# Final scatters of layer 2 moved to the pass boundaries, and the records' chain moved into the layer-0 block

## What is computed

```python
def _L0_gnn_ref(x, edge_index, edge_attr, W1, b1, W2, b2, Ws, bs, Wn, bn):
    h = relu(edge_attr @ W1.T + b1);  w = h @ W2.T + b2
    agg = segment_sum(w * x[src], dst)
    return relu(x @ Ws.T + bs + agg @ Wn.T + bn)

def _L1_gnn_ref(x, edge_index):                 # K = 10
    for _ in range(K):
        out = segment_sum(out[col] * w[:, None], row) * BETA + h * ALPHA
    return out / theta

def _L2_gnn_ref(x, edge_index):                 # K = 16, with self loops
    for _ in range(K):
        h = (1.0 - ALPHA) * segment_sum(norm * h[row], col) + ALPHA * x
    return h

def _L3_gnn_ref(x, edge_index, W1, b1, W2, b2, prelu_a):
    h = prelu(gcn_conv(x, W1, b1));  return prelu(gcn_conv(h, W2, b2))
```

## Time and profile before

| what | us |
|---|---|
| median of three runs | 11760.09 (11758.58 to 11783.25) |
| the profiled execution | 11771.36, span 11769.3 |
| PE busy | 4162.7 (35%) |
| DVE busy | 4557.7 (39%) |
| ACT busy | 3757.8 (32%) |
| POOL busy | 7378.6 (63%) |
| granted TensorE clock, mean | 0.561 |

### The profile page before, as it was taken

One profiled execution on the slowest core, in us unless ns is written; L12 is line 12 of the kernel. 1 busy time (PEld: TensorE's weight loads), 2 busy tenths in 40 slices (PEclk: granted clock), 3 DMA queues, 4 the chain that ended last, 5 costly groups with the idle time before them and its releaser, 6 DMA issues. The chain is left out here.

```text
span 11769.3 us, 85659 instructions
## 1 busy us (share of the span) xinstructions
PE 4162.7 (35%) x18774; PEld 3132.2 (27%) x18774; DVE 4557.7 (39%) x11458; ACT 3757.8 (32%) x11422; POOL 7378.6 (63%) x7464
## 2 busy tenths in 40 slices
PE   6860134333333333310333433333333332213433
PEld 4640033222222222210222222222222221112432
DVE  6970033333333334530344444444444432333334
ACT  6960034322222222363322222232222221143322
POOL 6877742666666666655566666666666666654455
PEclk8765555555555555555555555555555555555555
DMA  6561114333333333331333333333333332222211
GB/s 116 155 124 14 28 39 72 85 87 89 91 89 84 88 87 86 85 87 40 80 90 89 91 89 90 93 96 93 96 94 93 93 93 71 67 57 55 59 34 31
DMA packets 904311, 941.00 MB, mean 80 GB/s; under 512 B 378210, under 2 KB 789500, under 8 KB 903708
## 3 DMA queue, kind: packets, MB, share of 16 engines
q1 hardware_dynamic: 677870, 612.09, 17.8%
q0 software_dynamic: 225792, 323.35, 14.8%
q10 hardware_dynamic: 144, 0.10, 0.0%
HBM read 553.87 MB, written 408.86 MB: 82 GB/s over the span
## 5 line engine op out<-in xcount | busy, mean ns | idle before, releaser
L1655 POOL DMA_INDIRECT l_g<-tab,l x4704 | 4624.9, 983 | 2554.7 <-issue 1367.5
L1855 DVE TENSOR_TENSOR_SCAN l_w<-l_m,l_w,bank 96x512 f32<-96x512 bf16 x1248 | 1590.2, 1274 | 4380.1 <-remote 2758.8
L1692 PE MATMUL bank<-ident,l_w 96*128 96x96 f32 x5096 | 1089.1, 363 | 2419.3 <-DVE l_w L1855 1992.3
L1755 ACT ACTIVATE l_o<-l_o,coef_d 128x96 f32<-128x96 f32 x2940 | 856.7, 363 | 3187.2 <-DVE l_o L1883 1603.1
L1681 PE MATMUL bank<-ident,l_g 128*96 128x128 f32 x5096 | 1257.0, 396 | 1360.9 <-DMA l_g<-tab,l 603.1
L1692 PEld LDWEIGHTS bank<-ident,l_w 96*128 96x128 f32 x5096 | 844.8, 222 | 2714.3 <-DVE l_w L1855 2163.8
L1681 PEld LDWEIGHTS bank<-ident,l_g 128*96 128x96 f32 x5096 | 906.9, 189 | 1740.0 <-DMA l_g<-tab,l 645.1
L1751 ACT ACTIVATE l_o<-bank,coef_s 128x96 f32<-128x96 f32 x1764 | 452.4, 345 | 1838.2 <-remote 1114.1
L275 PE MATMUL bank<-tail_up,v 96*96 96x500 f32 (+1 forms) x298 | 296.3, 1098 | 1168.5 <-issue 944.2
L312 PE MATMUL bank<-ident,tail_up 96*125 96x96 f32 (+1 forms) x596 | 159.3, 422 | 780.6 <-issue 468.6
L1891 DVE TENSOR_TENSOR T<-l_o,XS 128x384 f32<-128x384 f32 x735 | 401.2, 546 | 10.7 <-ACT l_o L1755 10.7
(11 more groups left out here) (300 smaller groups left out, 10134.7 us busy)
## 6 DMA issues: line engine op xcount, KB each, us to landing
tab<-l_o SPq DMA_DIRECT2D x1176, 192.0 KB
l_g<-tab,l POOLq DMA_INDIRECT x4704
l_m<-mask_d SPq DMA_DIRECT2D x784, 96.0 KB
l_m<-mask_s SPq DMA_DIRECT2D x490, 96.0 KB
x3t<-XS SPq DMA_DIRECT2D x98, 192.0 KB
XM<-in_x_dram SPq DMA_DIRECT2D x100, 187.5 KB
x_meta<-in_x_dram SPq DMA_DIRECT2D x25, 750.0 KB
x1t<-XM SPq DMA_DIRECT2D x100, 187.5 KB
```

Source lines behind the costliest of these rows:

```text
L1655: nc.gpsimd.indirect_dma_start(out=tile(G[q % RG], t), out_offset=None, in_=tables[0:table_at + (2 - p % 2) * TR, :] if p else first, in_o ...
L1692: last = nc.tensor.transpose(b_bank(q)[:, u * D:(u + 1) * D], W[q % RW][:, u:GE:U], self.ident[0:D, 0:D])
L1755: last = a.activation(tile(O[q % RO], t), tile(O[q % RO], t), ACT.Copy, scale=self.coef_d[:, t:t + 1])
L1855: v.tensor_tensor_scan(out=W[q % RW][:, :], data0=masks[q % RM][:, :], data1=a_bank(q)[0:D, :], initial=W[(q - 1) % RW][:, GE - 1:GE] if q ...
```

## The change

**Lots.** There are now 13 lots: one of a single group (4 scatters) and twelve of four groups (16 scatters). Lot k is sent at the boundary ahead of smooth pass 4 + k, the last after the final group. None is sent inside a pass. Each is loaded at g = 40 of the pass before (the first at group 46 of pass 3, the last at group 8 of pass 15), by SP, after a wait until the scatters of the lot before and the tail job that it needs are done. The buffer is a part of `XM`, which now lives until the passes end; `XS` is another part of it.

**Tails.** `SLOTS` goes from 40 to 48, so a pass of 49 groups holds tail work nearly to its end. The 906 slots then end in the 19th pass that has tails (smooth pass 9) instead of the 23rd (smooth pass 13).

**Records.** The second half is made at g = 2 instead of 12. The block `load_records` goes. Its transfers stand in the block of the layer-0 sums: SP loads the records at g = 40 of its own loop, stores the keys at 42, loads them shifted at 44 and stores the mask at 47, DVE copies and compares at 41 and 46, and computes the targets behind its loop. A small block behind it holds eight casts and copies on DVE and POOL's clearing of semaphores. The power passes wait for the mask store (`order_masked`) before their first mask load.

```diff
-HALF, FIRST = 25, 12
+HALF, FIRST = 25, 2
+RECORDS_AT = 40
 PERIOD = 6
-SLOTS = 40
+SLOTS = 48
-LOT = 28
-LOT_SENT = ((14, 0), (14, 16), (14, 32), (15, 0), ...)
+LOT_GROUPS = 4
+LOTS = (1,) + (LOT_GROUPS,) * 12
+LOT_SENT = tuple(range(4, 17))
+LOT_LOADED = ((3, 46),) + tuple((p - 1, 40) for p in LOT_SENT[1:-1]) + ((15, 8),)
...
+                def order(step):
+                        if step == 0:
+                            scattered(sp)
+                            sp.dma_start(got[:, :, :].rearrange("p (g u) f -> p g (u f)", u=U),
+                                         self.rec.rearrange("(g p u) f -> p g (u f)", p=P, u=U)).then_inc(got_in, 16)
+                        if step == 2:
+                            sp.wait_ge(keyed, 1)
+                            sp.dma_start(slots_of(self.keys[0:TR]), by_group(key[:, :])).then_inc(written, 16)
+                        if step == 4:
+                            sp.wait_ge(written, 32)
+                            sp.dma_start(by_group(after[:, :]), slots_of(self.keys[1:TR + 1])).then_inc(shifted, 16)
+                        if step == 7:
+                            sp.wait_ge(linked, 1)
+                            sp.dma_start(slots_of(self.mask_s[1:TR + 1]), by_group(cont[:, :])).then_inc(self.order_masked, 16)
...
-                for g in range(NGP + 5):
+                for g in range(max(NGP + 5, RECORDS_AT + 8)):
                     if g < NGP:
                         load_mask(g)
+                    if g >= RECORDS_AT:
+                        order(g - RECORDS_AT)
...
+                    if g == RECORDS_AT + 1:
+                        dve.wait_ge(got_in, 16)
+                        v.tensor_copy(key[:, :], got[:, :, R_KEY]).then_inc(keyed, 1)
+                    if g == RECORDS_AT + 6:
+                        dve.wait_ge(shifted, 16)
+                        dve.wait_ge(keyed, 1)
+                        v.tensor_tensor(out=cont[:, :], in0=key[:, :], in1=after[:, :], op=ALU.is_equal).then_inc(linked, 1)
...
             def send_lot(pool, k):
+                a, b = lot_groups(k)
                 pool.wait_ge(lot_in, 16 * (k + 1))
-                for t in range(k * LOT, min((k + 1) * LOT, NT)):
+                for t in range(a * U, b * U):
...
-                        if smooth and (p, 0) in LOT_SENT:
-                            send_lot(pool, LOT_SENT.index((p, 0)))
+                        if smooth and p in LOT_SENT:
+                            send_lot(pool, LOT_SENT.index(p))
                         for r in range(RO):
                             pool.wait_ge(stored[r].sem, stored[r].at + 16 * stores_before(r, p * NGP))
                     for g in range(NGP):
-                        if smooth and g and (p, g) in LOT_SENT:
-                            send_lot(pool, LOT_SENT.index((p, g)))
...
+                if power:
+                    sp.wait_ge(self.order_masked, 32)
```

More of the change, by code:

```diff
@@ L453, in build @@
         self.outc = self.dram("outc", [TR, D])
+        parts = [self.rest[:, k * NT:(k + 1) * NT] for k in range(MF)]
+        self.col_i, self.own1 = (x.bitcast(i32) for x in parts[0:2])
+        self.l1 = [x.bitcast(i32) for x in parts[2:4]]
+        self.col_c, self.coef_s, self.lcoef, self.icoef = parts[4:8]
         with ExitStack() as s:
@@ L470, in build @@
             self.prepare()
-        self.XS = sb("XS", [P, NT * D])
         with ExitStack() as s:
             self.tails = Tail(self, s)
[L474 to L485, removed]
+            self.passes("l1", "power")
             self.passes("l2", "smooth")
@@ L1157, in prepare @@
             masked = [self.local(f"prep_masked{k}") for k in range(MR)]
-            block = s.enter_context(nc.Block())
+            key, after = tmp("key_s", [P, NT]), tmp("next_s", [P, NT])
+            cont = tmp("cont_s", [P, NT], bf16)
+            pad, none = tmp("pad_s", [1, U]), tmp("none_s", [1, 1], bf16)
+            seg = tmp("seg_c", [P, NT]), tmp("seg_e", [P, NT])
+            got = ms
+            got_in, keyed, written, shifted, linked = (
+                self.local(f"order_{n}") for n in ("landed", "keyed", "written", "shifted", "linked"))
             def cols(x, g):
@@ L1167, in by_row, with scattered @@
                 return x.rearrange("p (u d) -> p u d", d=D)
+            def scattered(eng):
+                for q in range(3 * NGP - RG, 3 * NGP):
+                    eng.wait_ge(self.fills(q), self.full(q))
+            stage = s.enter_context(ExitStack())
+            block = stage.enter_context(nc.Block())
             @block.gpsimd
@@ L1194, in _ @@
                             oob_is_err=False).then_inc(self.fills(q), 16)
-                for q in range(3 * NGP - RG, 3 * NGP):
-                    pool.wait_ge(self.fills(q), self.full(q))
+                scattered(pool)
             @block.sync
@@ L1572, in passes @@
                 split = self.sem("own_split")
-                lot = tmp("lot", [P, LOT * D])
+                lot = self.rest[:, 0:LOT_GROUPS * GD]
                 lot_in, lot_out = self.sem("lot_in"), self.sem("lot_out")
```

124 lines of the change are left out of this document (49 added, 75 removed).

## The result

The changed kernel took 11905.7 us (median of four runs, 11900.3 to 11915.9), the kernel before, on the same chip, 11771.7. The ratio is 1.0118, 95% interval 1.0104 to 1.0133. So it is slower by 134 us where I had forecast 26, and it lies above the range.

What follows compares the result with a forecast made beforehand. POOL's gather chain plus the drain of stores was taken as the bound. Terms −55 (records) −146 (lots) +161 +11 (boundary scatters) +55 (tails) = +26 gave 11786 us; range 11630 to 11855 for 8 in 10.

Steps and rivals of the forecast that it cites:

- What bounds the kernel: Whole period: POOL's chain of gathers, one every 1.25 us, plus the drain of stores behind it.
- Part 3: Scatters at pass boundaries: 16 at each of eleven, partly hidden by the drain, +161 us; 4 at a twelfth, +11.
- with three of five scans done and two left: Boundaries with 16 scatters: state of the drain when POOL stops at 20.7 us, leading to 37 us each, 43 with tails.
- The tails: Tails in 48 slots: denser groups and joins in the drain, +55 us, bounds 0 and +70; boundary joins 5.4 each besides.
- The four covered boundaries: Power-pass boundaries where own-row gathers cover the drain (0.31 us idle): longer tails cost +6 us together.
- The passes that lose their tails: POOL-bound passes without tails after the change: gain nothing, since 245 of the 277.8 us are pitch.
- Part 1: Records' chain before layer 1: own block gone −53, earlier half −20, delayed masks +18; −55 us, bounds −75 and −30.
- 1625 + 6 until the first: Layer-0 sums: scans resume 6 us after the record scatters end, 43 groups left, ending at 1844; gain 20 us.
- Part 2: Lots leaving the middle of smooth passes 14 (−79 us) and 15 (−67): −146, bounds −115 and −165.
- R3: Eleven boundaries: nothing drains beneath the scatters, more transfers precede the stores; 495 us instead of 437, 11844; chance 0.15.
- R2: Passes with tails: denser tails cost nothing, their matmuls find idle PE time; 87 us less, 11699; chance 0.15.
- R1: Eleven boundaries: scatters vanish in the wait for stores, −45 instead of +161 us; 11580, or 11640; chance 0.15.

Runs made afterwards that it cites:

- a_nolots: Changed kernel without the scatters at the twelve boundaries (180 of 196 tiles left out): 11697.1 us, ratio 0.9937 to the kernel before.
- b_slots48: Kernel before with only SLOTS raised from 40 to 48: 11936.6 us against 11772.2, ratio 1.0137.
- a_first12: Changed kernel with the second half of the records made after 12 scans again: 11926.9 us, ratio 1.0129 to the kernel before.
- after_again: Changed kernel unaltered, run again in a set without stalls: 10201.2 us against 10159.8 for the kernel before, ratio 1.0039.
- a_busy: Changed kernel with a POOL memset in place of each of 180 left-out scatters: 11712.8 us, ratio 0.995 to the kernel before.

## Why the prediction was wrong, step by step

**What bounds the kernel** was right: POOL's pitch plus the drain. The forecast missed by 108 us (+134 measured, +26 forecast), and most of that lies in the drain. By the table above the eleven boundaries took 65 us more than I had, the power passes 37 and the early smooth ones 10. The records' part lost another 20, and the passes between the boundaries gave back 24 that I had at nothing.

**Part 3, the scatters at the boundaries: right mechanism, too small.** The step that failed is "with three of five scans done and two left". I read from one boundary with 28 scatters that three scans come through in the first 20.7 us. The first of those began 0.2 us behind the first scatter (9710.72), and at the other such boundary only two were through in that time, both begun within 6 us (10117.45 and 10122.67). The scans of the changed kernel at its last boundary, where the last gather ended at 10322.83:

```profile
10328.67 1.28 DVE L1863 TENSOR_TENSOR_SCAN l_w<-l_m,l_w,bank 96x512 f32<-96x512 bf16 x1 [9.83 <-remote]
...
10346.25 1.27 DVE L1863 TENSOR_TENSOR_SCAN l_w<-l_m,l_w,bank 96x512 f32<-96x512 bf16 x1 [15.39 <-remote]
...
10348.36 1.27 DVE L1863 TENSOR_TENSOR_SCAN l_w<-l_m,l_w,bank 96x512 f32<-96x512 bf16 x1
...
10357.90 1.28 DVE L1863 TENSOR_TENSOR_SCAN l_w<-l_m,l_w,bank 96x512 f32<-96x512 bf16 x1 [1.04 <-PE bank L1689]
```

One scan at +5.8, then 15.39 us idle, and the next at +23.4, 2.6 us behind the last scatter. With it the drain begins: six scans. It is the same at the other five boundaries without tails: one scan through, four to six left. At the five with tails six are left and none comes through, but for one at +0.1 and one at +1.4. The six boundaries without tails last 41.6 us on average, against 20.7 in `a_nolots`: the difference is 20.9, the scatters' own time. The five with tails last 51.5 against 31.1. The term of 16 scatters was 17.2 each (37 less 19.8) and measured 20.4 to 20.9. The eleven sum to 507 us; the bound that I had named, 46 each if nothing comes through, is 506.

**The tails: the term that was mis-sized most.** Forecast with the joins 55 + 32 = 87, measured alone 164 (`b_slots48`). Two steps failed. In smooth passes I charged one join, 5.4 us. The drain with tails, from the boundary that ends at 7140.95:

```profile
7114.68 1.28 DVE L1863 TENSOR_TENSOR_SCAN l_w<-l_m,l_w,bank 96x512 f32<-96x512 bf16 x1 [24.29 <-remote]
...
7118.89 1.27 DVE L1863 TENSOR_TENSOR_SCAN l_w<-l_m,l_w,bank 96x512 f32<-96x512 bf16 x1
...
7126.39 1.28 DVE L1863 TENSOR_TENSOR_SCAN l_w<-l_m,l_w,bank 96x512 f32<-96x512 bf16 x1 [3.65 <-PE bank L1689]
...
7131.97 1.28 DVE L1863 TENSOR_TENSOR_SCAN l_w<-l_m,l_w,bank 96x512 f32<-96x512 bf16 x1
```

The join is there (7118.89 to 7126.39, 7.5 us). But it is not all: 3.5 us to the last scan instead of 3.2, 9.0 instead of 7.3 from the last scan to the gather, and six scans always, where plain boundaries have four to six. Without scatters (`a_nolots`) these boundaries last 30 to 34 us, where I had 25. In power passes I wrote +6 for the four boundaries where own-row gathers "cover the drain (0.31 us of idle)". The 0.31 was no margin. The 25 gathers covered a drain of one scan (3539.09, the only one behind the last gather at that boundary). With eight more slots of tails five are left, two of them come through beneath the gathers and three are left when they end, and the wait is 18.01 us at that same boundary (49.6 against 32.9). The four covered boundaries, +6 together in the forecast, cost +66. In sum the nine power boundaries cost +110, give or take the 19 us by which two traces of the kernel before differ there, and 38 came back in the passes.

The passes that lose their tails, to which I gave nothing "since 245 of the 277.8 us are pitch", gained 3.4 us each on average (smooth passes 9 to 13: 1381 us in sum where the kernel before has 1398).

**Part 1, the records: the step "1625 + 6 until the first" failed.** The scatters, the scans beneath them, and the last scan, which answer to the earlier trace rows:

```profile
L1202 POOL DMA_INDIRECT rec<-edge_record,record_row x196: 982/1095/1771, 1363.3 to 1636.8; - x196
...
L1368 DVE TENSOR_TENSOR_SCAN prep_at<-prep_mask,prep_at,bank x6: 1275/1276/1277, 1407.3 to 1651.9; 96x512 f32<-96x512 bf16 x6
...
1884.01 1.27 DVE L1368 TENSOR_TENSOR_SCAN prep_at<-prep_mask,prep_at,bank 96x512 f32<-96x512 bf16 x1 [13.74 <-DMA prep_mask<-mask_d]
```

The last scatter starts at 1636.8, not at 1624.4: they stand 1.40 us apart on average, where those of the kernel before stood 1.35 apart, the long wait left out. Beneath them the scans stood 49 us apart on average, and they didn't start again at once: one at 1651.9, the next 13 us behind it, where I had the first at 1631. So the stretch at 4.95 us began 34 us late, with 40 scans to go instead of 43. The last waits 13.74 us for its mask, the size that I had; another, behind the keys' store, waits 10.0 (at 1846.98), where I had 5 as cost. SP's queue shows why, and POOL's first gather behind it answers to the earlier trace rows:

```profile
1861.09 0.37 SPq L1235 DMA_DIRECT2D mask_s<-cont_s  x1
1863.94 11.38 SPq L1248 DMA_DIRECT2D x1t<-T  x1
1875.37 0.52 SPq L1249 DMA_DIRECT2D tab<-XM  x1
1875.93 0.64 SPq L1218 DMA_DIRECT2D prep_mask<-mask_d  x1
...
1915.76 0.99 POOL L1663 DMA_INDIRECT l_g<-x1t,XM  x1 [277.94 <-issue]
```

Behind the mask store at 1861.09 SP issues one store of the sums, which takes 11.38 us to issue, and only then, at 1875.93, the last mask. From the last scan to the gather 31.8 us remain (I had 33). So the gather comes at 1915.8 and not at 1895 because the scans end 22 us late: the gain is 34.5, and by `a_first12` 6 to 12 of it are the earlier half's, where I had 20. The bound of −30 that I gave this part was itself wrong by its own terms: 45 less 26 of cover is a cost of 19, and −53 −7 +19 is −41, which the −34.5 lies above. The rule of the Trainium skill ("DMA: Bandwidth & Descriptors", section "Two DMAs through the same engine are not ordered"), by which a later mask might overtake the store, did not apply: SP had not even issued the mask until the stores ahead of it were out.

**Part 2** held within 6 us in each of its two terms.

**The rivals.** R3 was nearest, 11844. Its condition, fewer than one of five scans through when POOL stops, holds at three of the five boundaries with tails and is just missed at those without. It still fell short, because the tails stood in it at my price; with the 77 us missing there it would have been 11921. R2 looked for the error of the tails on the wrong side. I had given the upper bound of the tails as +70, from intervals inside one DVE-bound pass, without a row of a drain that has tails to its end. R1's sign, no wait behind the scatters, is what the chips without stalls show, at another price.

## What to carry to other kernels

Where a wait for stores ends a pass, count everything that is still in the pipeline when the last gather is sent: filling the last free slots with background work moves that work into the drain, and a cover that just hides the drain has no margin to give. Work is not free just because its engine is idle; put the same length of another operation in its place (a memset for a DMA) and see which of the two holds the others. Put extra DMAs where another engine sets the pace, few at a time: two a group in two passes gave 0.9965, four a group in one of them 1.0063, on chips without stalls; with stalls only the former ran.

## What the runs showed of the hardware

On the chips with stalls a handoff by semaphore seems to wait for POOL's indirect DMAs. The clearest place is a chain on DVE alone, each step waiting for the semaphore of the one before. The changed kernel on a chip with stalls, DVE and then POOL:

```profile
1379.14 0.32 DVE L1483 TENSOR_TENSOR work<-meta_s,work 128x96 f32<-128x96 f32 x1 [1.20 <-DVE work L1482]
1380.54 0.26 DVE L1484 TENSOR_TENSOR work<-work 128x96 f32<-128x96 f32 x1 [1.08 <-DVE work L1483]
1381.94 0.33 DVE L1485 TENSOR_TENSOR edge_record<-work 128x96 f32<-128x96 f32 x1 [1.14 <-DVE work L1484]
1383.34 0.25 DVE L1487 TENSOR_SCALAR work<-XM 128x96 f32<-128x96 f32 x1 [1.07 <-DVE edge_record L1485]
...
1379.47 1.09 POOL L1202 DMA_INDIRECT rec<-edge_record,record_row  x1 [0.31 <-issue]
1380.86 1.09 POOL L1202 DMA_INDIRECT rec<-edge_record,record_row  x1 [0.30 <-issue]
```

The operations take 0.3 us and start 1.40 us apart, which is just the distance of POOL's DMAs. The same instructions in `after_again`, without stalls:

```profile
1348.33 0.32 DVE L1483 TENSOR_TENSOR work<-meta_s,work 128x96 f32<-128x96 f32 x1
1348.69 0.26 DVE L1484 TENSOR_TENSOR work<-work 128x96 f32<-128x96 f32 x1
1348.98 0.39 DVE L1485 TENSOR_TENSOR edge_record<-work 128x96 f32<-128x96 f32 x1
1349.41 0.25 DVE L1487 TENSOR_SCALAR work<-XM 128x96 f32<-128x96 f32 x1
...
1347.73 0.98 POOL L1202 DMA_INDIRECT rec<-edge_record,record_row  x1 [0.30 <-issue]
1349.01 0.98 POOL L1202 DMA_INDIRECT rec<-edge_record,record_row  x1 [0.30 <-issue]
```

There they start 0.29 to 0.43 apart, with POOL issuing every 1.28 us. The scans of the sums beneath the same scatters, whose like stood 49 us apart in the changed kernel with stalls:

```profile
L1368 DVE TENSOR_TENSOR_SCAN prep_at<-prep_mask,prep_at,bank x39: 1275/1276/1278, 1356.9 to 1549.7; 96x512 f32<-96x512 bf16 x39
```

That is one each 5.1 us. A pass needs several handoffs per group (turn, scan, turn back, sum, scale, add, store), and beneath scatters in a row DVE sat idle for 13.97 us ahead of a scan in the earlier trace rows, and for 15.39 in the changed kernel. The Trainium skill, "Perfetto Trace Analysis", section "Per-engine timelines", says that a semaphore update travels on after the recorded end and that this time is not in the profile. The gaps in these rows would fit it: they grow from under 0.1 us to 1.1. The trace doesn't show which part of the handoff takes them. POOL's memsets (`a_busy`) don't do this, only its indirect DMAs.

The size of it was not expected: the same program takes 11761 us in one set and 10160 in another, 14% less, with POOL's gathers at a median of 944 to 947 ns in both. The gathers of a pass of the changed kernel take 275 to 282 us in the one and 245 to 256 in the other, smooth passes 0 and 15 left out. The TensorE clock isn't what differs: its mean was granted at 0.557 in the trace with stalls and at 0.549, no higher, in the one without. Why sets differ is open. It is not simply the chip, as far as the record's numbers go, since number 5 appears in both conditions. A cost holds for the condition in which it was read: the change is 1.2% slower with stalls and 0.4% without.
